# Silu on ScalarE in place of Tanh in a cross-attention and mixture-of-experts kernel

## What is computed

```python
# layer 0: 9 experts of width 352, all computed, weighted with cw (zero but for the top two)
h = silu(x_flat @ ew1[e].T) * (x_flat @ ew3[e].T)
out = out + cw[:, e:e + 1] * (h @ ew2[e].T)
# layer 1: 8 experts of width 176, and a shared one weighted with sigmoid(sg)
eo = einsum('eti,eih->eth', silu(g) * u, w_down)
out = einsum('te,eth->th', combine, eo) + sg * (silu(x @ sw_gate) * (x @ sw_up) @ sw_down)
```

## Time and profile before

| what | value |
|---|---|
| median of 3 runs | 1862.99 us (1861.21 to 1863.65) |
| the profiled execution's own time | 1860.5 us |
| its span, first to last instruction | 1858.8 us |
| mean granted TensorE clock | 0.979 |
| TensorE busy | 1646.0 us, 89% |
| VectorE busy | 1207.0 us, 65% |
| ScalarE busy | 899.6 us, 48% |
| GpSimd busy | 631.2 us, 34% |

### The profile page before, as it was taken

One profiled execution on the slowest core, in us unless ns is written; L12 is line 12 of the kernel. 1 busy time (PEld: TensorE's weight loads), 2 busy tenths in 40 slices (PEclk: granted clock), 3 DMA queues, 4 the chain that ended last, 5 costly groups with the idle time before them and its releaser, 6 DMA issues.

```text
span 1858.8 us, 36224 instructions
## 1 busy us (share of the span) xinstructions
PE 1646.0 (89%) x13858; PEld 903.6 (49%) x13858; DVE 1207.0 (65%) x2626; ACT 899.6 (48%) x2024; POOL 631.2 (34%) x1059
## 2 busy tenths in 40 slices
PE   4159999889998999899998999989999999989999
PEld 3113655337452474435653375534745356543655
DVE  4058556867478564895658765685748956588555
ACT  4138433672427534384335834276343853458333
POOL 3325223441324214352243513253142522345123
PEclk9579999999999999999999999999999999999999
DMA  7410140002200041000400023000311004000130
GB/s 213 78 33 2 27 59 14 22 1 45 41 16 19 6 66 24 26 2 16 70 14 22 2 38 47 17 19 6 59 24 33 2 5 79 15 22 2 32 53 16
DMA packets 56155, 59.87 MB, mean 32 GB/s; under 512 B 6436, under 2 KB 44208, under 8 KB 55984
## 3 DMA queue, kind: packets, MB, share of 16 engines
q1 hardware_dynamic: 55984, 57.57, 15.7%
HBM read 43.67 MB, written 13.88 MB: 31 GB/s over the span
## 4 chain that ended last, share of the span: by engine, by line
PE 69%; DVE 11%; ACT 6%; issue 6%; POOL 4%; DMA 3%; SPq 1%; another core or an unknown queue 0%; POOLq 0%
PE ob L700 7%; PE ob L503 7%; PE b L488 6%; PE a L687 6%; PE a L688 6%; DVE mx L1054 4%; PE a L401 4%; PE a L464 4%; PE b L473 4%; PE a L583 3%; PE ob L401 3%; PE a L582 3%; ACT probs L848 3%; PE b L694 2%; DMA k_parts<-big 2%
## 5 line engine op out<-in xcount | busy, mean ns | idle before, releaser
L1054 DVE TENSOR_REDUCE mx<-a 128x2 f32<-128x802 f32 (+1 forms) x512 | 494.8, 990 | 122.7 <-PE a L464 111.8
L848 ACT ACTIVATE probs<-b 128x512 f32<-128x512 f32 (+1 forms) x896 | 452.9, 567 | 42.0 <-PE b L488 35.1
L503 PE MATMUL ob<-probs,vaug 128*9 128x256 f32 (+1 forms) x3328 | 276.1, 384 | 17.7 <-ACT oT L810 17.7
L917 ACT ACTIVATE big<-a 128x256 f32<-128x256 f32 (+2 forms) x304 | 116.7, 384 | 304.6 <-PE a L688 303.9
L1276 POOL TENSOR_TENSOR big<-iotab,idx_lo 128x512 bf16<-128x512 bf16 x256 | 258.3, 1041 | 5.0
L464 PE MATMUL a<-kst,qa 64*128 64x401 bf16 (+1 forms) x1024 | 172.2, 340 | 50.0 <-SPq L326 45.7
L488 PE MATMUL b<-sq_nat,kst 64*128 64x256 bf16 (+1 forms) x1664 | 171.7, 279 | 19.8 <-ACT probs L848 10.1
L1146 DVE SCALAR_TENSOR_TENSOR big<-big,a 128x256 f32<-128x256 f32 (+2 forms) x304 | 127.0, 418 | 85.4 <-ACT big L917 84.1
L1232 POOL TENSOR_TENSOR rstd<-veps,neg_half 128x2 f32<-128x2 f32 x33 | 23.3, 706 | 361.0 <-DVE veps L965 361.0
L1265 POOL CAST qst<-nm 128x4 bf16<-128x4 f32 x64 | 13.0, 203 | 388.8 <-DVE nm L1038 388.8
L488 PEld LDWEIGHTS b<-sq_nat,kst 64*128 64x128 bf16 (+1 forms) x1664 | 51.1, 95 | 181.4 <-ACT probs L848 168.6
(11 more groups left out here) (220 smaller groups left out, 2651.4 us busy)
## 6 DMA issues: line engine op xcount, KB each, us to landing
kst<-k_parts SPq DMA_DIRECT2D x108, 200.1 KB
k_parts<-big SPq DMA_DIRECT2D x27, 400.2 KB, 14.0
ctx_sb<-in_ctx SPq DMA_DIRECT2D x10, 768.0 KB
k1st<-k_parts SPq DMA_DIRECT2D x108, 32.0 KB
k_parts<-kpart SPq DMA_DIRECT2D x27, 64.0 KB, 2.0
kst<-in_L_ffn_w SPq DMA_DIRECT2D x1, 1408.0 KB
x<-in_x SPq DMA_DIRECT2D x9, 128.0 KB, 2.2
out<-x SPq DMA_DIRECT2D x8, 128.0 KB, 1.8
```

The lines of the kernel that those rows point to most:

```text
L503: m = pe.matmul(ob[q:q + V1, 0:NQ], vaug[0:kn, c, 2 * p + hh, :], probs[0:kn, (2 * g + hh) % NPS, (c % 2) * NQ:(c % 2 + 1) * NQ], start=(j ...
L848: act.activation(probs[0:kn, n % NPS, 0:w], bs[e % 3][0:kn, 0:w], ACT.Exp).then_inc(b_read, 1)
L1054: dve.tensor_reduce(mx[:, p % 2, s, :, j], (a0, a1)[k % 2][:, :].rearrange("p (h k) -> p h k", h=2)[:, :, 0:n], AX, ALU.max, negate=True). ...
```

## The change

ScalarE takes Silu of the gate straight from its PSUM bank into `th`. VectorE's step (th + 1) * gate is left out, and with it the tile `gt` and the semaphore gt_done. VectorE multiplies `th` with up. The factors of 0.5 and 2 in the routing become 1.

```diff
-        th, gt, hu = (big[:, 5632 + 768 * k:5632 + 768 * (k + 1)].rearrange("p (n q) -> p n q", q=NQ) for k in range(3))
+        th, hu = (big[:, 5632 + 768 * k:5632 + 768 * (k + 1)].rearrange("p (n q) -> p n q", q=NQ) for k in range(2))
@@ ScalarE, experts
                     if c >= 3:
-                        act.wait_ge(gt_done[l], c - 2)
-                    act.activation(th[0:n, c % 3, :], gu_bank[c % 3][0:n, 0:NQ], ACT.Tanh, scale=0.5).then_inc(th_ready[l], 1)
+                        act.wait_ge(hu_done[l], c - 2)
+                    act.activation(th[0:n, c % 3, :], gu_bank[c % 3][0:n, 0:NQ], ACT.Silu).then_inc(th_ready[l], 1)
@@ VectorE, routing
-                    st.do(dve.tensor_scalar(lz[:, :, 8:9], le[:, :, 8:9], 1.0, 2.0, ALU.add, ALU.mult))
+                    st.do(dve.tensor_scalar(lz[:, :, 8:9], le[:, :, 8:9], 1.0, None, ALU.add))
-                st.do(dve.scalar_tensor_tensor(out=wtop[:, :, :], in0=top[:, :, 0:2], scalar=0.5, in1=wrec[:, :].unsqueeze(2).to_broadcast([P, NS, 2]),
+                st.do(dve.scalar_tensor_tensor(out=wtop[:, :, :], in0=top[:, :, 0:2], scalar=1.0, in1=wrec[:, :].unsqueeze(2).to_broadcast([P, NS, 2]),
@@ VectorE, experts
                     dve.wait_ge(th_ready[l], c + 1)
-                    dve.scalar_tensor_tensor(out=gt[0:n, c % 3, :], in0=th[0:n, c % 3, :], scalar=1.0, in1=g[0:n, 0:NQ],
-                                             op0=ALU.add, op1=ALU.mult).then_inc(gt_done[l], 1)
                     if c == 0:
                         dve.wait_ge(cwT_psum[l], 1)
                         dve.tensor_copy(cwT[:, :], bsb[0][0:CWR, 0:NQ]).then_inc(cwT_ready[l], 1)
                     if c >= 1:
                         hidden(c - 1)
-                    dve.wait_ge(gt_done[l], c + 1)
-                    dve.tensor_tensor(hu[0:n, c % 3, :], gt[0:n, c % 3, :], g[0:n, NQ:2 * NQ], ALU.mult).then_inc(hu_done[l], 1)
+                    dve.tensor_tensor(hu[0:n, c % 3, :], th[0:n, c % 3, :], g[0:n, NQ:2 * NQ], ALU.mult).then_inc(hu_done[l], 1)
```

More of the change, by code:

```diff
@@ L193, in build @@
             [sem(f"{n}{k}") for k in range(2)] for n in ("gate_psum", "lz_ready", "le_ready", "cwp_ready", "cwT_psum", "cwT_ready"))
-        gu_ready, th_ready, gt_done, hu_done, cb_ready, hid_ready, down_done = (
-            [sem(f"{n}{k}") for k in range(2)] for n in ("gu_ready", "th_ready", "gt_done", "hu_done", "cb_ready", "hid_ready", "down_done"))
+        gu_ready, th_ready, hu_done, cb_ready, hid_ready, down_done = (
+            [sem(f"{n}{k}") for k in range(2)] for n in ("gu_ready", "th_ready", "hu_done", "cb_ready", "hid_ready", "down_done"))
         ctxT_psum, ctxT_ready, side_psum, side_act = (sem(n) for n in ("ctxT_psum", "ctxT_ready", "side_psum", "side_act"))
```

## The result

The changed kernel takes 1868.91 us (median of 12 runs, 1865.97 to 1883.41), the kernel before 1863.08 us (12 runs, 1860.88 to 1863.65). The ratio is 1.004, with a 95% interval of 1.0023 to 1.0057: slower by 5.8 us, where I had put a gain of 2.3 us as likeliest. The profiled execution of after took 1869.23 us with a span of 1867.4 us, 8.6 us longer than that of before. The granted clock fell from a mean of 0.979 to 0.969, and the changed kernel's times spread more widely.

A forecast was written before the change was run, and what follows sets the result against it. TensorE, busy for 89% of the span, was taken as the bound. Edge gains of 8.3 us less 6.0 us of table loads gave -2.3 us on the 1862.99 us median: 1860.7 us, range 1853.7 to 1869 us.

The forecast's parts named there:

- The middle of the loops is hidden: Mid-loop in the expert layers TensorE sets the pace, so nearly all of the removed VectorE step's 127.0 us is hidden.
- Layer 0, start and tail: Edges of layer 0's expert loop: gains of 0.33 us a round at the start and 0.34 us at the tail.
- Layer 1: Expert layer 1: nothing at start or tail, but the whole 0.37 us idle before `weights(3)` goes each round.
- The table loads: Switches between Exp and Silu on ScalarE: 31 loads, hidden except before attention 0's first Exp, seven times 0.85 us, 6.0 us.
- Case A: The forecast: Silu in another table, each load running ahead of the Exp's wait; 1860.7 us, own range 1857 to 1864, chance 0.44.
- B: As Case A, but a load sits between the Exp's wait and the Exp in attention; 1865.6 us, chance 0.22.
- C: A table switch stalls ScalarE for 2.57 us, twice the row, by emptying and restarting; 1873.7 us, chance 0.17.
- D: Silu shares Exp's table, so there are no loads; 1854.7 us, chance 0.14.
- E: Silu's table lacks Identity or Copy, giving ten more loads a round in layer 0; tens of microseconds slower, chance 0.03.
- the sentence that passes a load's delay on as 0.85 us and nothing more: Attention 0: scores, maxima and next queries form one chain, so the first Exp's full 0.85 us delay passes on, seven times.

The follow-up runs named there:

- the filled kernels: Idle matmuls in TensorE's waits at attention 0's start, four kernels: before 1861.61 us; changed 1860.99; changed, load at round start, 1856.12; Tanh without VectorE's step 1856.63.
- the run with three idle matmuls: The changed kernel with three idle matmuls between the first and second group of scores in attention 0, table load left in place; 1861.58 us, ratio 1.0001.
- early load, four more matmuls: The changed kernel with a one-column Exp moving the table load to the round's start, plus four idle matmuls ahead of layer 1's expert loop; 1862.19 us.

## Why the prediction was wrong, by its steps

**The middle of the loops is hidden.** Right. A round with 38 steps of 0.42 us less on VectorE gained 0.76 us.

**Layer 0, start and tail.** Right: 0.33 us and 0.34 us, as predicted.

**Layer 1.** The mechanism was there, the size was not: 0.14 us for 0.37 at `weights(3)`, and 0.08 us lost at the start, where I had written that there is nothing to gain. This term of the sum was too large by 0.3 us a round. I took the idle time of a weight load for idle time of the array. Eight rounds give about 6.1 us, not 8.3.

**The table loads.** Right in number (31), place (ahead of the wait), cover (all but attention 0) and price (0.83 us in the trace, 0.86 us in the filled kernels, 0.85 predicted). Case A was the case that happened, though its own range ended at 1864 us; B, C, D and E did not. So the undisturbed round should be 218.07 - 0.76 + 0.86 = 218.17 us, 0.1 us longer than before and not 0.2 us shorter, and the run with three idle matmuls showed 218.15 to 218.20. Here the account of instructions ends, and it comes out even.

**What was missing: TensorE's clock.** The step that failed is the sentence that passes a load's delay on as 0.85 us and nothing more: what a longer wait does to TensorE's clock stood at nothing in the sum, without a reason. Seven undisturbed rounds of 218.17 us are 1527.2 us; after took 1538.7 us, an excess of 11.5 us, with the two slow stretches towards the end of attention 0 in it. Before: 1526.5 us and 1529.0 us, an excess of 2.5 us. The difference of 9.0 us, with 0.7 us for the rounds and -1.1 us for the first, is the 8.6 us between the spans.

The profile of before had the rows for it: TensorE's granted clock was below 1.00 at attention 0 in two of seven rounds, at waits that the change lengthens (0.96 us to about 1.8 us at the second group of scores). That the longer wait does it here is read from two kernels whose undisturbed rounds are equally long: with the old waits (early load, four more matmuls, 218.18 us) two rounds of seven have a slow stretch, with the load's wait (the changed kernel, 218.17 us) all seven. Taking the load away did not give the gain back: the rounds are then 0.76 us shorter, and even the old waits bring a slow stretch in seven and in six of seven.

I read the mean clock of 0.979, named no stretch of it, and had no rival in which the clock decides. The range, 1853.7 to 1869 us, held the median by 0.1 us, and only because case B's bound reached that far. B did not occur, so that was luck.

What stays open: which of the waits in attention 0 matters most was not tried one by one, by what rule the chip picks the moment was not measured, and the slow stretches 85 us and 148 us into a round were not followed up.

## What to carry to other kernels

Ask of a new function on ScalarE whether it shares its table with those around it, look where ScalarE is idle before the switch back, and put a one-column activation of the next function there. Before pricing a change of some microseconds, read the granted clock of each stage and each round, not its mean: waits of TensorE that cost nothing in one round cost over a microsecond in the next, and a kernel that gets shorter can lose its gain there. An idle time on a weight load bounds a gain from above; the distance to the next matmul that could not start says what is real.

## What the runs showed of the hardware

A table load takes 1.28 us, starts as soon as ScalarE's last instruction ends, even when the activation behind it still waits, and needs no further time: the Exp starts 1.29 us after the load. TensorE's clock fell to its lower level in one round and not in the next, with the same instructions and the same waits, and adding 0.85 us of matmuls a round elsewhere removed five of seven such falls (one execution of each kernel). One fall at attention 0 cost 1.1 to 1.4 us in the kernel before; in the changed kernel a round exceeded its 218.17 us by 1.1 to 2.4 us, two of the seven with a second fall. A fall elsewhere cost 2.7 us.
